# Where a score round waits for its PSUM banks, and where seven of them serve it, in a two-block transformer kernel

## What is computed

```python
x = _L0_xcond_ref(...)   # attention 1 (windows), attention 2 (top 16), SwiGLU
# block 1, _L1_xcond_ref:
h = layernorm(x, ln1_g, ln1_b)
h = mha(h, h, ...)                       # attention 3: 1024 x 1024 scores per head
x = x + h + t_sa[:, None, :]
h = layernorm(x, ln3_g, ln3_b)
h = mha(h, context_emb, ..., mask=mask)  # attention 4: 1024 x 154 scores per head
x = x + h + t_ca[:, None, :]
h = layernorm(x, ln2_g, ln2_b)
h = gelu(h @ w1 + b1) @ w2 + b2
# in mha:
scores = einsum('bqhd,bkhd->bhqk', q, k) / np.sqrt(HD)
attn = softmax(scores)
out = einsum('bhqk,bkhd->bqhd', attn, v) @ wo + bo
```

## Time and profile before

| | |
|---|---|
| median of 3 runs | 1604.16 us (1602.31 to 1604.68) |
| the profiled execution's own time | 1604.09 us |
| its span (first to last instruction) | 1602.3 us |
| PE, DVE, ACT, POOL busy | 89%, 57%, 45%, 21% |
| attention 3 | about 616 to 1278 us |
| attention 4 with its token steps | about 1278 to 1447 us |

### The profile page before, as it was taken

The page is one execution under the profiler, slowest core; times in us unless marked ns, Lnnn a source line. Parts: engine busy times, 40 slices in busy tenths (PEclk is TensorE's granted clock), DMA queues, the critical chain, the costliest instruction groups (busy, mean ns, idle before and its releaser), DMA issues.

```text
span 1602.3 us, 25438 instructions
## 1 busy us (share of the span) xinstructions
PE 1422.4 (89%) x9100; PEld 696.2 (43%) x9100; DVE 919.3 (57%) x2815; ACT 715.2 (45%) x1454; POOL 341.7 (21%) x377
## 2 busy tenths in 40 slices
PE   5999877768969787789989999999999998998898
PEld 3567654434634444234223433333333254544565
DVE  2455569977767885665556666667576154440111
ACT  2245445555444352214554465555455843433221
POOL 0011067865655662100000000000010000010110
PEclk9899968899979899899999999999999999999999
DMA  5022100000000001000002000000000000000000
GB/s 179 1 86 82 52 1 14 8 1 1 5 1 1 28 1 36 0 1 1 1 1 67 1 1 1 1 1 2 1 11 1 1 2 1 12 5 7 7 23 20
DMA packets 22092, 26.74 MB, mean 17 GB/s; under 512 B 4204, under 2 KB 19634, under 8 KB 21708
## 3 DMA queue, kind: packets, MB, share of 16 engines
q1 hardware_dynamic: 21059, 25.03, 4.9%
q10 hardware_dynamic: 909, 0.10, 0.0%
HBM read 21.58 MB, written 3.08 MB: 15 GB/s over the span
## 4 chain that ended last, share of the span: by engine, by line
PE 76%; DVE 11%; ACT 6%; issue 4%; POOL 2%; DMA 0%; ACTq 0%; SPq 0%; DVEq 0%; POOLq 0%
PE bank L943 28%; PE bank L900 10%; PE bank L983 8%; PE bank L915 7%; PE bank L879 6%; PE bank L858 3%; PE bank L1007 2%; DVE x_hat L1361 2%; PE bank L837 2%; PE bank L865 1%; DVE left L1416 1%; PE bank L1026 1%; PE bank L885 1%; DVE top L1413 1%; DVE left L1423 1%
## 5 line engine op out<-in xcount | busy, mean ns | idle before, releaser
L1173 ACT ACTIVATE pr<-bank 128x512 f32<-128x512 f32 x656 | 355.0, 597 | 350.0 <-PE bank L943 349.9
L1388 DVE TENSOR_REDUCE part_max<-bank 128x1 f32<-128x512 f32 x512 | 327.6, 685 | 199.8 <-PE bank L943 198.9
L943 PE MATMUL bank<-slot 32*128 32x512 f32 (+1 forms) x3072 | 396.0, 524 | 6.4 <-ACT pr L1173 4.8
L943 PEld LDWEIGHTS bank<-slot 32*128 32x128 f32 x3072 | 156.5, 186 | 222.5 <-issue 169.6
L1438 POOL TENSOR_SCALAR var_eps<-mean_var 128x4 f32<-128x4 f32 x24 | 5.5, 227 | 1024.1 <-DVE mean_var L1352 1023.9
L1494 POOL TENSOR_SCALAR left<-left 128x308 f32<-128x308 f32 x128 | 125.4, 979 | 115.6 <-ACT exp_all L1195 47.1
L900 PE MATMUL bank<-h_t,w_m 128*128 128x512 f32 x256 | 131.6, 638 | 19.9 <-ACT hidden L1149 13.3
L983 PE MATMUL bank<-pr,v 128*17 128x512 f32 x1024 | 135.4, 601 | 0.0
L1496 POOL TENSOR_TENSOR probs<-left,exp_all 128x308 f32<-128x308 f32 x128 | 107.1, 837 | 10.6
L1413 DVE MAX8 top<-bank 128x8 f32<-128x154 f32 x256 | 69.7, 314 | 57.7 <-PE bank L1007 45.9
L1195 ACT ACTIVATE exp_all<-bank,neg 128x154 f32<-128x154 f32 x256 | 85.6, 387 | 9.6 <-DVE left L1416 5.9
(11 more groups left out here) (140 smaller groups left out, 1847.0 us busy)
## 6 DMA issues: line engine op xcount, KB each, us to landing
w_m<-in_L_xcond_w_m SPq DMA_DIRECT2D x1, 2048.0 KB, 8.8
w_m<-in_L_xcond_w_m SPq DMA_DIRECT2D x2, 1024.0 KB, 6.9
w<-in_L_xcond_w SPq DMA_DIRECT2D x2, 1024.0 KB, 6.4
w_ada<-in_L_xcond_w_ada SPq DMA_DIRECT2D x1, 1792.0 KB, 10.7
x_sb<-in_x SPq DMA_DIRECT2D x6, 256.0 KB, 7.3
res_row<-rows_dram SPq DMA_DIRECT2D x12, 128.0 KB, 3.3
out_x<-x_sb SPq DMA_DIRECT2D x6, 256.0 KB, 2.1
wa<-in_L_xcond_w_qkv SPq DMA_DIRECT2D x1, 768.0 KB, 8.1
```

Source lines behind the costliest of these rows:

```text
L943: last = nc.tensor.matmul(g.bank(*tile)[:, into], left, right, start=True, stop=True)
L1173: nc.scalar.activation(m.pr[:, u % NPR, :], g.bank("s", gi, i)[:, :], ACT.Exp).then_inc(g.free("s", gi, i), 1)
L1388: nc.vector.tensor_reduce(m.part_max[:, slot, h * TB + i // 8, i // 4 % 2:i // 4 % 2 + 1], bank[:, :], axis=AX.X, op=ALU.max).then_inc(don ...
```

## The change

Three edits. First, `scores` waits for the banks of all its tiles ahead of its first product; before, each tile's wait stood at that tile's own first product. This holds in attentions 1, 3 and 4. Second, the 12 slots of stage (5, 0) are dealt out over the odd rounds 163 to 191, so that they stand at rounds 163 to 189 with two odd rounds left empty between them; before, they stood at every fourth odd round or so, from 163 to 249. Third, the tiles `m`, `m_turn` and `s` of groups 22 and 23 and the `s` tiles of group 21, which begin when those slots are over, may use bank 0 as well, so seven banks.

```diff
 def banks_of(step):
     kind = step[0]
     if kind in ("m", "m_turn", "s"):
+        if step[1] in (22, 23) or step[0] == "s" and step[1] == 21:
+            return (0, 1, 2, 3, 4, 5, 6)
         return (1, 2, 3, 4, 5, 6) if attention(step[1]) == 3 else (3, 4, 5, 6)
...
-    where = plan.fill(joined([gap_slots(5, 0, n) for n in range(2)]), [gaps[c] for c in range(163, 256, 2)])
+    where = plan.fill(joined([gap_slots(5, 0, n) for n in range(2)]), [gaps[c] for c in range(163, 192, 2)])
     plan.at(where[-1] + 0.1, ("load_row", 8), ("load_out", 6))
...
         elif kind == "scores":
             tiles = step[1:]
+            for tile in tiles:
+                for signal in g.emptied(*tile):
+                    since(pe, signal)
             for j in range(4):
                 for tile in tiles:
                     if j == 0:
-                        for signal in g.emptied(*tile):
-                            since(pe, signal)
                         at, gi, i = attention(tile[1]), tile[1], tile[2]
```

## The result

The changed kernel takes 1652.78 us (1652.21 to 1662.14, 4 runs) against 1604.42 us: 1.0315 times the kernel before, 95% interval 1.0276 to 1.0354. The forecast was 1608.6 us with a range to 1614.0. The sign is right, the size is wrong by more than a factor of ten: 48 us instead of 4.5. Several kernels of this text, the kernel before among them (in one batch 7 of 19 executions at 1614 to 1618 us), have some executions 8 to 15 us above their others, so medians are compared.

The account below looks back on a forecast made before the run. PE was taken to set the pace, with 76% of the chain, though it waits for banks in some rounds. 0.4 + 1.3 + 4.8 + 3.0 - 3.7 - 1.3 = +4.5 us on 1604.09 gave 1608.6, range 1601.0 to 1614.0.

Parts of the forecast that it names:

- nil: Attention 1: no tile was ever ready before the fourth bank, so edit 1 costs nothing, at most 0.5 us either way.
- 0.4 + 1.3 = 1.7: Attention 3, edit 1: 0.4 us over some 20 plain pairs, 1.3 us at late banks of round A.
- 3.0 - 3.7 - 1.3 = -2.0: Dense slots cost 3.0 us net; seven banks save 3.7 in plain pairs and 1.3 in rounds of `s` alone.
- 4.8: Attention 4, edit 1: held products make rounds late, 4.8 us together, bounds 1 and 8.
- the clock: Rival: the lower clock level returns in ten places of plain pairs and attention 4, about 1 us each; 1618.6 us, chance 0.06.
- the count of ten: Attention 4: ten rounds without a token step of PE's to cover the wait lose 0.30 to 0.76 us each.
- the forecast 4.00 and 3.86: Plain pairs of rounds in attention 3 after the change: 4.00 us with six banks, 3.86 with seven.
- only five places: Attention 3 before stage (5, 0): five late banks of round A followed by a plain round B, 1.3 us in all.
- the move alone: -0.5: Dense slots: three slots no longer share their place with an output's turn, net 0.5 us saved.
- -3.7 - 1.3 = -5.0: Seven banks: 0.12 us gained in each of 31 pairs, 0.22 in each of six pairs of `s` rounds.
- the 31 counted: Pairs from the end of the dense slots that seven banks would shorten by 0.12 us each, 3.7 us together.
- The rival in which the halves cancel: Attention 4 and the dense part each give back half of their loss; +0.6 us, 1604.7 us, chance 0.27.

Follow-up runs that it names:

- e13: Kernel before plus the common wait in attention 4 alone, with overwritten filler products over all 128 rows ahead of 17 rounds; 1612.08 us (1.0075).
- e6: Kernel before plus the common wait in attention 3 only, with spread slots and six banks; 1622.22 us (1.0110).
- e1: Kernel before plus edit 1 alone, with spread slots and six banks; 1667.57 us (1.0378).
- e5: Kernel before plus the common wait in attention 1 only; executions of 1608.48 to 1624.25 us, median 1.0074 times the kernel before.
- e14: Changed kernel with a round's banks waited for from last tile to first; median 1637.91 us (1.0218).
- e15: Changed kernel, but rounds with a tile of attention 4 keep each product's own wait; 1631.42 us (1.0164).
- e8: Kernel before plus edit 3 alone, with spread slots and own waits; 1606.35 us (1.0014).
- e2: Kernel before plus edits 2 and 3, without the common wait; 1607.49 us (1.0007).

## Why the prediction was wrong, by its own steps

The forecast beside the profiled executions, us:

| rounds | forecast | measured |
|---|---|---|
| 1 to 33, attention 1 | nil | 6.9 |
| 37 to 185 | 0.4 + 1.3 = 1.7 | 9.7 |
| 185 to 300 | 3.0 - 3.7 - 1.3 = -2.0 | 6.8 |
| 300 to 345, attention 4 | 4.8 | 25.6 |
| the rest | nil | -0.9 |

Two steps failed: the clock was put at nothing, and edit 1 was priced far too low in attention 3. Either alone would have brought the time above the range. The direction was right.

**Attention 4 without the clock was about right.** Rounds wait as the forecast said: the full-height product comes late, and `pv` behind it. The lateness there was forecast as 4.8 us; the stretch grew by at least 4.5 beside the clock, and e13 leaves 6.8. The steps that the count of ten missed are the rounds behind an `m_turn`: their last tile has the bank of the turn, and the whole round now waits for its copy, 0.46 to 0.56 us idle where there was none, in six rounds of attention 4.

**The first step that failed is the clock's.** It stood as a rival with a chance of 0.06, at ten places of 1 us in attentions 3 and 4. It fell in attention 4, by up to 21.5 us, and in attention 1, hardly in the plain pairs; over the run it made up to 25.5. Two sentences led astray. "Attention 3 as a whole had 0.98 with single waits of up to 1 us" was used for all stages, but attention 3 kept its clock through the waits of edit 1 (e6) and told nothing on attention 4, whose rounds carry less work between waits. And the price of one fall was taken from one round, 2.09 instead of 1.14. What stands behind that round is doubled too: behind one fall of the changed kernel, 7.0 us went by for what takes 3.6.

**Attention 1: "nil" was wrong.** That all four banks are wanted within the first tenths of a round is true, and the round behind an `m_turn` still starts 0.54 late, for the turn's copy; with others of this kind 2 us, and 5 of clock. In the profiled executions of e1, e5, e14 and e15 the stretch behind it was 9 to 11 us longer at a clock of 0.85, with the same instructions; in that of the changed kernel it was not. One run of the changed kernel (1662.14) stands as far off without a profile.

**The second is edit 1 in attention 3.** With spread slots and nothing else changed it costs 18 us at an unchanged clock (e6), four times the whole forecast. A plain pair was to cost 0.02 us and measured 0.11; the 0.09 are the semaphore instruction (e14 gives the forecast 4.00 and 3.86). Pairs with late banks cost as forecast in kind (5.52 for 5.05 at a y_mm) but were more numerous: 9.7 us up to round 185 against 1.7, of which some 2 by clock and 2 by the 0.09. In the rounds of `s` alone edit 1 costs 0.39 a pair with six banks (e6), which the sum left out. That only each late bank's own length counts held; that only five places had one did not.

**Edit 2** was to cost 3.0 net with edit 1's waits. By itself it costs 1.5 (forecast for the move alone: -0.5). Together with edit 3 and on top of edit 1 it gained 9.3 us in rounds 185 to 300 (e1 against the changed kernel), where 3.0 - 5.0 = -2.0 was forecast; no run parts the two there. The 46 pairs, forecast at 203.7, lasted 1266.99 - 1056.61 = 210.4:

```profile
1056.61 1.14 PE L946 MATMUL bank<-slot 32*128 32x512 f32 x8
1266.99 1.14 PE L946 MATMUL bank<-slot 32*128 32x512 f32 x8
```

In the slot with a qk and two turns the pair is 8.58 instead of 10.1, as no fall of the clock follows it.

**Edit 3** was -3.7 - 1.3 = -5.0. The plain pairs gained 0.14, more than the 0.12 forecast, but of the 31 counted 23 came out plain at 3.95; the others hold a turn or follow a late bank. The pair of `s` rounds is 0.07 below the kernel before and not 0.22, and the cost of bank 0 to the output's turn was never priced: three turns at 0.96 and one at 0.6. That token steps take bank 0 if it is empty was known; what was left out was to ask who waits for bank 0 when a score has it. Measured without edit 1: -2.6 in rounds 185 to 285 with spread slots (e8), nothing with dense ones.

The rival in which the halves cancel gives nearly the time of edits 2 and 3 alone (e2), but it was about edit 1's losses being given back, and they were not.

## What to carry to other kernels

Where PE fills waits with parts of a round, as here in attention 4, moving them can cost the clock, so look at the granted clock stage by stage and price a wait at its own length plus what the work behind it takes longer at the lower level. Count every round whose last bank can be late, not only the plain case: here these were the larger part. If several semaphores must be waited for at one instruction, put the one that comes last on the instruction itself. Before a buffer is opened to a second user, look at what its first user would then wait for: four output turns that had cost nothing took back all that a seventh bank gained with dense slots.

## What the runs showed of the hardware that was not expected

- Several semaphores at one product: besides the one that it waits for itself there are instructions of 0.051 us on PE's queue (806 instead of 176), and with the last bank behind one of them the product started 0.15 us after it was empty instead of 0.06 (pairs of 4.09 and 4.00).
- Products in one of four row groups did not keep TensorE at 2.4 GHz in attention 4 (0.91), products over all 128 rows did (0.99), at the same places and with the same number.
- A stage of 434 us without a changed instruction came out 9 to 11 us longer, at a granted clock of 0.85 for 0.88, in the profiled executions of four kernels (e1, e5, e14, e15) that have the common wait in attention 1. It probably makes most of the 15 us between 1608.5 and 1624.0 for one and the same kernel (e5), of which only the slower kind has a profile. Whether the common wait is its cause is not shown: the kernel before and others without that wait also have executions some 12 us above the rest, none of them profiled.
